# Five fewer matmuls on zeros at the head, and the small constants loaded behind the first piece of x

## The chip, the cores and the metric

The kernel runs on one core of a Trainium2 chip. Its time is the device time in microseconds (us) of one execution, and the median of several executions is compared. Five engines work side by side and meet only at semaphores: PE (TensorE, matrix products), DVE (VectorE), ACT (ScalarE), POOL (GpSimd) and SP (SyncE, which here only issues DMAs).

## What is computed

The input x is 1024 tokens of 512 float32 values. Two residual steps follow each other:

```python
x = x + attn(cond(x, itok_B_0_7, cond_W, cond_Wr, cond_A, cond_B), ...)
x = x + ffn(cond2(x, itok_B_0_23, cond2_W, cond2_b, lora_As, lora_Bs), ...)
```

`cond` is the stage that matters here. It computes the plain product `base = x @ W.T`, and beside it router logits `x @ Wr.T` with a bias for the language id of the batch, keeps the two largest of eight experts, and adds their rank-16 updates, weighted by a softmax, to `base`. `attn` is a polynomial approximation plus a gated feed-forward, `cond2` a product with an adapter chosen by id, and `ffn` a second gated feed-forward with low-rank parts. All of it is float32.

## The kernel before

The tokens are cut into two halves of 512 columns. x lies transposed in chunks of 128 channels, so the tile `X` has eight pieces, called here x00 to x03 for the first half and x10 to x13 for the second, each 128x512 float32 (256 KB). The weight of `cond` comes in four pieces of the same size, w0 to w3, one for each chunk of channels.

Every float32 operand is split into a high part, copied by ACT into a rounded format, and a low part, which DVE makes by subtracting the high part from the original. A product then takes three matmuls (low times high, high times low, high times high). ACT and DVE thus stand between every DMA and every matmul: a piece lands, ACT copies it, DVE subtracts, PE may use it. All copies carry line 541 and all subtractions line 911, since helpers record them.

The order at the head is written out by hand in the list `FIRST` (line 66): x00, w0, x01, x02, x03, w1, x10, x11, w2, x12, x13, w3. Three engines follow it in order. SP issues the loads in this order, from line 470 on. ACT makes the high parts in this order (line 567), with one addition: right behind the two copies of w0 it waits for `small_in`, the semaphore of the tile `sm`, and copies the router weight `WR` out of `sm` (lines 576 and 577). DVE makes the low parts in the same order, with `WR` in the same place (line 986). Only then do both go on to x01.

POOL issues three loads of small constants as the first things it does: `sm` (128 rows of 191 values, 95.5 KB; router weight, bias, identity matrix and more), `idb` (language ids, 4 KB) and `slot_i` (adapter ids). Its next instruction waits for `slots_ok` (line 500), which DVE makes out of `slot_i` at line 1006.

PE begins with `WARM` matmuls of 128x128 in bfloat16 on a tile of zeros (line 1502), which need only the memset of line 974. Their results are used by nobody. Then follow `base_0(0)` (12 matmuls on x00 and w0; the first three at lines 1510, 1512 and 1514), the logits of the first half (seven matmuls, lines 1455, 1458 and 1453, which need `WR` and x00 to x03), `base_0(1)` (12 matmuls on x01 and w1), the logits of the second half, and so on. The matmuls of `product` stand at lines 1435, 1436 and 1437. The core of PE's order at the head:

```python
base_0(0)
pe.wait_ge(wr_ready, 1)
for k in range(KC):
    pe.wait_ge(x_ready, x_count(0, k))
    logits(0, k)
base_0(1)
```

`base_0(1)` waits for `w_ready`, which DVE raises with the low part of w1.

Of the kernel before, what the change touches and what calls it, by code (L numbers as in the profile page):

```python
# [37 lines left out]
P_AP = P_GATE + 1  # L38
P_FFN = P_AP + 1 + ORDERS
RING = 4  # L40
WARM = 39


KS = 96
# [120 lines left out]
def build(nc, x, ids_b, slot_ids, small, pieces, parts, lora_a, lora_b, stk_up, out):  # L165
    with ExitStack() as ctx:
# [3 lines left out]
        def sem(name):  # L170
            return ctx.enter_context(nc.semaphore(name))
# [82 lines left out]
        x_in = [[sem(f"x_in{h}{c}") for c in range(KC)] for h in range(HALVES)]  # L254
# [82 lines left out]
        def raw_slot(p):  # L337
            k = (0, 1, 6, 7, 2, 3)[SLOT[p]]
            return raw[:, k, :]

        def raw_count(p):
            return 16 * SLOT[:p + 1].count(SLOT[p])

        def before_in_slot(p):

            return max([q for q in range(p) if SLOT[q] == SLOT[p]] or [P_TWO[LAST - 1]])
# [52 lines left out]
        def sum_region(q):  # L399
            a = SUM_AT[q % 2]  # L400
            return raw_flat[:, a:a + 1024]

        def merge_region(q):
            a = 3072 * (q % 2)
            return raw_flat[:, a:a + 1024]

        def merged_by_dma(q):

            return q - F2 - 1
# [58 lines left out]
        @block.sync  # L468
        def _(sp):
            for kind, h, c in FIRST:  # L470
                if kind == "x":
                    sp.dma_start(X[:, h, c, :], x[h, c]).then_inc(x_in[h][c], 16)
                else:
                    sp.dma_start(raw_slot(P_CW + c), pieces[P_CW + c]).then_inc(raw_in[SLOT[P_CW + c]], 16)
            for p in range(RING, PIECES):
                k, q = BLOCK_PIECES[p - P_FFN] if P_FFN <= p < P_S13 else (None, None)
                if k == 1:
                    if q > 1:
                        sp.wait_ge(w_ready, P_TWO[q - 2] + 1)
                    sp.dma_start(sum_region(q), parts[q][:, 0:1024]).then_inc(sum_in[q % 2], 16)  # L480
                sp.wait_ge(w_ready, before_in_slot(p) + 1)
                if k == 0:
                    a11 = slice(256 * (q % 2), 256 * (q % 2) + 256)
                    sp.dma_start(raw_slot(p)[:, a11], pieces[p][:, a11]).then_inc(raw_in[SLOT[p]], 16)
                else:
                    sp.dma_start(raw_slot(p), pieces[p]).then_inc(raw_in[SLOT[p]], 16)
            for n, (h, c, cols, _) in enumerate(OUTPUTS):

                sp.wait_ge(out_ready, n + 1)
                sp.dma_start(out[h, c, :, cols], X[:, h, c, cols]).then_inc(out_done, 16)  # L490
            sp.wait_ge(out_done, 16 * len(OUTPUTS))


        @block.gpsimd
        def _(pool):
            pool.dma_start(sm[:], small).then_inc(small_in, 16)
            pool.dma_start(idb[:], ids_b).then_inc(ids_in, 16)
            pool.dma_start(slot_i[:], slot_ids).then_inc(slots_in, 16)

            pool.wait_ge(slots_ok, 1)  # L500
            for b in range(BATCH):
                s = pool.value_load(slot_ok[0:1, b:b + 1], min_val=0, max_val=SLOTS - 1)
                pool.dma_start(ga_raw[:, b * KC * RANK:(b + 1) * KC * RANK], lora_a[s]).then_inc(lora_a_in, 16)
            pool.dma_start(su_raw[:], stk_up[0]).then_inc(su_in, 16)

            def sums_by_dma(q):

                k, n, at = q % 2, q // 2 + 1, SUM_AT[q % 2]
                pool.wait_ge(sum_in[k], 16 * n)
                pool.dma_start(raw_flat[:, at:at + 768], parts[q][:, 1024:1792], accum_op=ALU.add).then_inc(sum_two[k], 16)  # L510

            for q in range(F2):
                sums_by_dma(q)
            pool.wait_ge(g_ready, G_SPLIT[0, TAIL - 1, "T4"])
            for b in range(BATCH):
                s = pool.value_load(slot_ok[0:1, b:b + 1], min_val=0, max_val=SLOTS - 1)
                for row in (b % TILES * RANK, KB + b % TILES * RANK):
                    pool.dma_start(gb_raw[row:row + RANK, b // TILES, :], lora_b[s]).then_inc(lora_b_in, 16)
            def su_load(q):
                pool.wait_ge(su_ready, q)  # L520
                pool.dma_start(su_raw[:], stk_up[q]).then_inc(su_in, 16)

            def merge_by_dma(q):
                for p in (P_ONE[q], P_TWO[q]):
                    pool.wait_ge(raw_in[SLOT[p]], raw_count(p))
                pool.wait_ge(delta_out, merged_by_dma(q))
                pool.dma_start(merge_region(q), delta[:], accum_op=ALU.add).then_inc(merged_in, 16)

            for q in range(1, 3):
                su_load(q)  # L530
            for q in range(F2 + 2, END + 1):
                if q in (F2 + 5, F2 + 9, F2 + 11):
                    su_load({F2 + 5: 3, F2 + 9: 4, F2 + 11: 5}[q])
                merge_by_dma(q)
# [897 lines left out]
        def _(pe):  # L1432
# [67 lines left out]
            pe.wait_ge(warm_ready, 1)  # L1500
            for _ in range(WARM):
                pe.matmul(PB[LOGITS[1]][:, 0:P], warm[:], warm[:], start=True, stop=True)  # L1502
# [436 lines left out]
```

## Time and profile before

| | us |
|---|---|
| median of 3 runs (439.1 to 440.13) | 439.77 |
| the profiled execution | 439.4 |
| its span, first to last instruction | 437.7 |
| PE busy | 433.9 (99% of the span) |
| DVE, ACT, POOL busy | 347.3, 242.1, 40.6 |

The profile is of one execution. Its span and its time differ by 1.7 us, which lie outside of the instructions. A row of the timeline gives the start of a group, the time from its start to its end, the engine, the line, the operation with its output and input, and the count; where the engine sat idle before, the idle time and what ended it stand in brackets. SPq and POOLq are the instruction queues of these engines. The busy time of PE comes from modelled ends of pipelined matmuls, which overlap; short waits of PE are therefore read from the distance of two starts and not from the busy time. A DMA's time to landing runs from its issue to the last of its semaphore increments.

### The profile page before, as it was taken

To read this page: it belongs to the slowest core of one execution; us is meant where nothing else is said; L and a number is where in the kernel's file an instruction comes from. 1 tells how busy PE (TensorE), PEld (TensorE's weight loads), DVE (VectorE), ACT (ScalarE), POOL (GpSimd) and SP (SyncE) were. 2 spreads that over 40 slices of the span, in tenths; PEclk is the share of its full clock that TensorE was granted. 3 is DMA by queue.
4 is the path that set the end of the run, shared out by engine and by line. 5 is a ranking of instruction groups with operands and counts; after the bars stand their busy time and mean duration, and the time that the engine had idled before them with its cause. 6 is when DMAs were issued, how large, how long until landed. Compare 5 with 4: busy or idle time off the path is not lost.

```text
span 437.7 us, 5667 instructions
## 1 busy us (share of the span) xinstructions
PE 433.9 (99%) x1969; PEld 357.2 (82%) x1969; DVE 347.3 (79%) x524; ACT 242.1 (55%) x364; POOL 40.6 (9%) x64
## 2 busy tenths in 40 slices
PE   8999999999999999999999999999999999999997
PEld 7788888888888888888888888888888888888886
DVE  4756699676888867987799589799988799988663
ACT  6455443427566446664574658586754566755520
POOL 1003200000000001003400000010001010010000
PEclk9999999999999999999999999999999999999999
DMA  8505800044555655565551024054645444444004
GB/s 276 166 0 155 234 16 1 9 123 104 130 126 130 175 131 128 130 152 144 156 171 49 18 67 97 0 121 98 146 89 137 121 105 107 96 97 100 21 13 180
DMA packets 22171, 47.26 MB, mean 108 GB/s; under 512 B 2880, under 2 KB 4944, under 8 KB 22144
## 3 DMA queue, kind: packets, MB, share of 16 engines
q1 hardware_dynamic: 16992, 32.51, 24.0%
q0 software_dynamic: 5152, 14.39, 17.9%
q8 instruction: 16, 0.26, 0.3%
q14 instruction: 11, 0.09, 0.1%
HBM read 37.98 MB, written 2.10 MB: 92 GB/s over the span
## 4 chain that ended last, share of the span: by engine, by line
PE 99%; DVE 0%; issue 0%; DVEq 0%
PE PS L1589 21%; PE PS L1591 21%; PE PS L1590 21%; PE PS L1435 10%; PE PS L1437 10%; PE PS L1436 10%; PE PS L1705 1%; PE PS L1502 1%; PE PS L1713 0%; PE PS L1455 0%; PE PS L1749 0%; PE PS L1765 0%; PE PS L1766 0%; PE PS L1453 0%; PE PS L1747 0%; PE PS L1722 0%
## 5 line engine op out<-in xcount | busy, mean ns | idle before, releaser
L1589 PE MATMUL PS<-HT,WU 128*128 128x512 f32 x294 | 114.9, 391 | 0.0
L1590 PE MATMUL PS<-HT,WU 128*128 128x512 f32 x294 | 114.5, 390 | 0.0
L1591 PE MATMUL PS<-HT,WU 128*128 128x512 f32 x294 | 114.4, 389 | 0.0
L541 ACT ACTIVATE WU<-raw 128x256 fp32r<-128x256 f32 (+2 forms) x60 | 56.4, 939 | 29.6 <-PE PS L1591 17.0
L911 DVE TENSOR_TENSOR WU<-raw,WU 128x256 fp32r<-128x256 f32 (+2 forms) x61 | 65.0, 1065 | 4.8 <-ACT WU L541 4.7
L541 ACT ACTIVATE PS<-PS 128x512 f32<-128x512 f32 x58 | 33.9, 584 | 61.8 <-PE PS L1591 38.7
L1589 PEld LDWEIGHTS PS<-HT,WU 128*128 128x128 f32 x294 | 55.2, 188 | 12.3 <-DVE PS L1114 1.0
L541 ACT ACTIVATE G<-T 128x512 fp32r<-128x512 f32 (+3 forms) x62 | 49.5, 810 | 28.2 <-DVE T L1152 14.0
L1591 PEld LDWEIGHTS PS<-HT,WU 128*128 128x128 f32 x294 | 55.2, 188 | 11.7
L1590 PEld LDWEIGHTS PS<-HT,WU 128*128 128x128 f32 x294 | 55.2, 188 | 11.0
L911 DVE TENSOR_TENSOR G<-T,G 128x512 fp32r<-128x512 f32 (+3 forms) x59 | 53.2, 914 | 12.3 <-ACT G L541 11.6
L1589 PE MATMUL PS<-G,WU 128*128 128x512 f32 x112 | 43.6, 389 | 0.0
L1590 PE MATMUL PS<-G,WU 128*128 128x512 f32 x112 | 43.6, 389 | 0.0
L1591 PE MATMUL PS<-G,WU 128*128 128x512 f32 x112 | 43.6, 389 | 0.0
L1118 DVE TENSOR_TENSOR T<-PS,T 128x512 f32<-128x512 f32 x29 | 19.9, 687 | 15.2 <-PE PS L1591 15.2
L696 ACT ACTIVATE T<-PS 128x512 f32<-128x512 f32 x42 | 24.9, 592 | 12.4 <-PE PS L1591 12.4
L1114 DVE TENSOR_TENSOR PS<-PS,T 128x512 f32<-128x512 f32 x29 | 20.2, 695 | 9.4 <-ACT T L541 7.4
L1435 PE MATMUL PS<-G,WU 128*128 128x512 f32 x68 | 26.5, 390 | 0.0
L1437 PE MATMUL PS<-G,WU 128*128 128x512 f32 x68 | 26.5, 389 | 0.0
L1436 PE MATMUL PS<-G,WU 128*128 128x512 f32 x68 | 26.5, 389 | 0.0
L510 POOL DMA_DIRECT2D raw<-in_parts x14 | 12.1, 863 | 145.5 <-DMA raw<-in_parts 145.5
L1591 PEld LDWEIGHTS PS<-G,WU 128*128 128x128 f32 x112 | 21.0, 188 | 4.4
(169 smaller groups left out, 694.5 us busy)
## 6 DMA issues: line engine op xcount, KB each, us to landing
raw<-in_pieces SPq DMA_DIRECT2D x73, 256.0 KB, 3.0
raw<-in_parts SPq DMA_DIRECT2D x14, 512.0 KB, 3.7
raw<-delta POOLq DMA_DIRECT2D x13, 512.0 KB, 5.5
raw<-in_parts POOLq DMA_DIRECT2D x14, 384.0 KB, 5.0
X<-in_x SPq DMA_DIRECT2D x8, 256.0 KB, 5.6
raw<-in_pieces SPq DMA_DIRECT2D x14, 128.0 KB, 2.5
out_x<-X SPq DMA_DIRECT2D x7, 256.0 KB, 2.0
su_raw<-in_stk_up POOLq DMA_DIRECT2D x6, 192.0 KB, 5.8
```

Of the source, the lines that this page charges most:

```text
L510: pool.dma_start(raw_flat[:, at:at + 768], parts[q][:, 1024:1792], accum_op=ALU.add).then_inc(sum_two[k], 16)
L541: return nc.scalar.activation(o, i, ACT.Copy)
L696: nc.scalar.activation(T[:, h, :], bank, ACT.Silu).then_inc(silu[h], 1)
L911: return V.tensor_tensor(dst, full, f32(hi), ALU.subtract)
L1114: V.tensor_tensor(bank_b(q), bank_b(q), T[:, 4, :], ALU.add).then_inc(added_b, 1)
L1118: V.tensor_tensor(T[:, 5, :], bank_c(q), T[:, 4, :], ALU.add).then_inc(added_d, 1)
L1435: pe.matmul(o, w[:, 1, cols], xx[:, 0, :], start=start, stop=False)
L1436: pe.matmul(o, w[:, 0, cols], xx[:, 1, :], start=False, stop=False)
L1437: return pe.matmul(o, w[:, 0, cols], xx[:, 0, :], start=False, stop=stop)
L1589: pe.matmul(bank, w[:, 1, cols], hi, start=start and kc == 0, stop=False, skip_group_check=not start)
L1590: pe.matmul(bank, w[:, 0, cols], low, start=False, stop=False, skip_group_check=not start)
L1591: mm = pe.matmul(bank, w[:, 0, cols], hi, start=False, stop=kc == 1, skip_group_check=not start)
```

## The change

PE makes 34 matmuls on zeros instead of 39. POOL waits for the landing of x00 before it issues the three loads of small constants. Nothing else differs.

```diff
-WARM = 39
+WARM = 34
@@
         @block.gpsimd
         def _(pool):
+
+            pool.wait_ge(x_in[0][0], 16)
             pool.dma_start(sm[:], small).then_inc(small_in, 16)
             pool.dma_start(idb[:], ids_b).then_inc(ids_in, 16)
             pool.dma_start(slot_i[:], slot_ids).then_inc(slots_in, 16)
```

## Rows read from the trace of the kernel before

**Rows 1.** The page: the chain that ended last, its share by engine.
```profile
PE 99%; DVE 0%; issue 0%; DVEq 0%
```

**Rows 2.** The timeline of PE, the head up to the second product.
```profile
1.11 4.34 PE L1502 MATMUL PS<-warm 128*128 128x128 bf16 x39 [1.11 <-DVE warm L974]
5.21 0.77 PE L1510 MATMUL PS<-HT,G 128*128 128x512 f32 x1
5.79 0.46 PE L1512 MATMUL PS<-HT,G 128*128 128x512 f32 x1
6.08 0.39 PE L1514 MATMUL PS<-HT,G 128*128 128x512 f32 x1
...
6.31 0.40 PE L1435 MATMUL PS<-HT,G 128*128 128x512 f32 x1
```

**Rows 3.** The timeline of PE, the last logits and the first matmuls of `base_0(1)`.
```profile
8.39 0.40 PE L1455 MATMUL PS<-HT,WR 128*16 128x512 f32 x1
...
9.79 0.39 PE L1453 MATMUL PS<-HT,WR 128*8 128x512 f32 x1
...
10.02 0.40 PE L1455 MATMUL PS<-HT,WR 128*16 128x512 f32 x1
...
10.30 0.47 PE L1435 MATMUL PS<-HT,G 128*128 128x512 f32 x1
```

**Rows 4.** The timeline of ACT, its copies at the head.
```profile
3.48 0.63 ACT L541 ACTIVATE HT<-X 128x512 fp32r<-128x512 f32 x1 [1.12 <-DMA X<-in_x]
4.25 0.31 ACT L541 ACTIVATE G<-raw 128x128 fp32r<-128x128 f32 x1
...
6.09 0.23 ACT L541 ACTIVATE WR<-sm 128x32 fp32r<-128x32 f32 x1 [1.11 <-DMA sm<-in_small]
6.86 1.88 ACT L541 ACTIVATE HT<-X 128x512 fp32r<-128x512 f32 x3 [0.54 <-DMA X<-in_x]
8.79 0.63 ACT L541 ACTIVATE G<-raw 128x512 fp32r<-128x512 f32 x1
```

**Rows 5.** The timeline of DVE, its subtractions at the head and the ids.
```profile
4.75 0.82 DVE L911 TENSOR_TENSOR G<-raw,G 128x128 fp32r<-128x128 f32 x2
6.35 0.19 DVE L911 TENSOR_TENSOR WR<-sm,WR 128x32 fp32r<-128x32 f32 x1 [0.79 <-ACT WR L541]
7.53 1.95 DVE L911 TENSOR_TENSOR HT<-X,HT 128x512 fp32r<-128x512 f32 x3 [0.98 <-ACT HT L541]
9.46 0.69 DVE L911 TENSOR_TENSOR G<-raw,G 128x512 fp32r<-128x512 f32 x1
12.15 1.38 DVE L911 TENSOR_TENSOR G<-X,G 128x512 fp32r<-128x512 f32 x2
14.12 0.17 DVE L989 CAST idf<-idb 128x8 f32<-128x8 int32 x1
33.76 0.15 DVE L1003 CAST slot_f<-slot_i 1x8 f32<-1x8 int32 x1
```

**Rows 6.** The timeline of POOL at the head, and its time to landing for `sm`.
```profile
1.42 0.70 POOL L496 DMA_DIRECT2D sm<-in_small  x1 [0.86 <-POOLq L1929]
2.12 0.58 POOL L497 DMA_DIRECT2D idb<-in_ids_b  x1
2.67 0.55 POOL L498 DMA_DIRECT2D slot_i<-in_slot_ids  x1
...
DMA to landing us min/median/max: 4.6/4.6/4.6
```

**Rows 7.** Issue to landing of later POOL loads: `in_lora_b`, `in_lora_a`, `in_stk_up` (32, 32, 192 KB).
```profile
DMA to landing us min/median/max: 1.9/2.6/4.5
...
DMA to landing us min/median/max: 2.2/2.9/5.9
...
DMA to landing us min/median/max: 2.6/5.8/6.6
```

**Rows 8.** Busy time by stretch; the last three columns are granted clock, DMA share, GB/s.
```profile
3.00:3.50 0.50, 0.50 (x8) 0.50 (x6) 0.00 (x0) 0.02 (x1) 0.22 (x1) 1.00 1.06 401
3.75:4.75 1.00, 1.00 (x12) 1.00 (x11) 0.61 (x2) 0.85 (x3) 0.00 (x0) 1.00 0.76 185
8.00:12.00 4.00, 4.00 (x19) 2.28 (x18) 4.00 (x7) 3.77 (x7) 0.00 (x0) 1.00 1.05 402
```

## The prediction

> **What bounds the kernel now.** I read the chain that ended last first. It is PE for 99% of the span [rows 1], so a microsecond in which PE has no work is a microsecond of the result, and one saved at the head stays saved only if PE's next operand is there as early. The edits touch the first ten microseconds alone, so I read those in the timeline, engine by engine.
>
> PE starts on zeros at 1.11 and its 39 matmuls end at 5.45; the first real one starts at 5.21, as the weights are loaded ahead, and the next at 5.79, 6.08 and 6.31 [rows 2]. (5.45 - 1.11 - 0.31 for the last one alone) over 38 distances is 0.106 us for 128 columns, which is the 1.2 GHz level. The starts of the 512-column matmuls are 0.57, 0.29 and 0.23 apart: 0.23 is the 2.4 GHz level, so the clock rises at about 5.9, within the second real matmul. (The column of the granted clock reads 1.00 for the head too [rows 8]; the distances contradict it there, and I go by them.) Then 0.23 apart all along, until the last logits matmul at 10.02. The next would start at 10.25, but starts at 10.30 [rows 3], because the low part of w1 is done only at 9.46 + 0.69 = 10.15 [rows 5]. So at this place PE and the split of w1 arrive together: whichever becomes later sets the start of `base_0(1)`. After it there is room: the low part of x13 ends at 13.53 [rows 5], while its logits matmuls follow the 12 of `base_0(1)` and five others, at 10.30 + 17 x 0.23 = 14.2.
>
> What makes w1 late? ACT copies it at 8.79 right behind x01, x02 and x03 (from 6.86), and before them it stood idle twice: 1.11 us for `sm`, until 6.09, and 0.54 us for x01 [rows 4]. The DMAs ran at 401 GB/s until POOL's loads came in and at 185 GB/s from 3.75 to 4.75, and at 402 again from 8 to 12 [rows 8]. This is what the second edit aims at.
>
> **Five matmuls fewer.** 5 x 0.106 = 0.53 us. The first real matmul would start at 5.21 - 0.53 = 4.68. Its inputs are there: the copy of w0's first part ends at 4.25 + 0.31 = 4.56 [rows 4]. But it now runs at the lower level: 128 columns take 0.106, so 512 take 0.43. Starts: 4.68, 4.68 + 0.57 = 5.25, 5.68; if the clock rises at 5.9 as before, the third is half done by then and the fourth starts at about 6.01 instead of 6.31. It needs the second part of w0, done at 4.75 + 0.82 = 5.57 [rows 5]. So 0.30 of the 0.53 us remain, PE is through with the logits at 9.95 instead of 10.25, and waits there for w1. Alone this edit is worth 0.00 to 0.05 us, since w1 at 10.15 covers it. The bounds of its worth with w1 out of the way are 0.30 and, had the clock risen before 4.7, 0.53.
>
> **The loads of the constants.** What moves is all three issues on POOL, 0.70, 0.58 and 0.55 us [rows 6]. x00 is there at 3.48, when ACT starts on it [rows 4]; with some 0.05 for the wait the issue of `sm` starts at 3.53 instead of 1.42, 2.1 later. `idb` and `slot_i` move as much. With the 4.6 us to landing of `sm`, `idb` landed at 6.7 and will at 8.8, and is wanted at 14.12; `slot_i` will at 9.4 and is wanted at 33.76 [rows 5, 6]; POOL itself has nothing else to do before `slots_ok`. What hides these two is the splitting of x and w on DVE, and they would cost only if they were some 5 us later than that. `sm` is not hidden: ACT stands at it in order, and x01, x02, x03 and w1 are queued behind it on ACT, then on DVE, and PE waits for these.
>
> The one unknown is `sm`'s time from issue to landing in its new place. It was 4.6 [rows 6]. POOL's later loads span 1.9 to 6.6 [rows 7]: 1.9 to 3 when little else moves, up to 5.9 for 32 KB when SP's loads run beside them. At 3.5 to 8 us SP's queue is as full as it was at 1.4 to 6, so I take 4.6, the nearest row by place, size and neighbours, and keep 2.6 to 5.9 for the range.
>
> Then `sm` lands at 3.53 + 4.6 = 8.15, and x01 to w1 have landed by then or soon after, as SP's queue ran free meanwhile. ACT copies `WR` from 8.18 and is at x01 at 8.18 + 0.26 = 8.44 (was 6.86). Three copies at the pace of (1.88 - 0.63) / 2 = 0.62 bring w1's copy to 10.30 and its end to 10.93, DVE's part ends 0.73 later, at 11.66 (the same 0.73 as from 9.42 to 10.15), and `base_0(1)` starts 0.15 later, at 11.8 instead of 10.30. That is +1.5 us. PE meanwhile ends `base_0(0)` at about 8.1 and then has only seven matmuls to do until 11.8, some 2 us idle in pieces. The part of DVE that follows keeps pace: five more subtractions at 0.69 [rows 5] bring x13 to 15.1, and it is wanted at 11.8 + 17 x 0.23 = 15.7. From there on PE is bound by itself as before, so the shift goes through to the end.
>
> In general the shift at `base_0(1)` is (time to landing - 4.6) + 1.5, and never below 9.95 - 10.30 = -0.35, where PE itself is the limit. The second edit swallows all that the first gives unless the landing takes under 3.1 us.
>
> **A rule weighed.** `sm` took 4.6 us for 95.5 KB [rows 6]. The Trainium skill, page "DMA: Bandwidth & Descriptors", section "Anatomy of one DMA", fits a load issued from GpSimd as 2.0 us plus its bytes over 436 GB/s; by it this one takes 2.2, an estimate, and lands at 5.8. This trace does not agree for a load with neighbours, and does for the fastest of the small ones (1.9 to 2.6). The case is the rival "quick landing" below, which is worked out from rows.
>
> **The rivals.**
> Quick landing (the other side: no loss or a gain). If POOL's load meets less traffic in its new place, it may land like the fastest later ones, 2.6 to 3 us [rows 7], at 6.1 to 6.5. ACT is at x01 by 6.4 to 6.8, w1's copy ends at 8.9 to 9.3 and `base_0(1)` can start at 9.8 to 10.2; PE arrives at 9.95. Shift -0.35 to -0.1, time 439.05 to 439.3. It needs w1 to have landed by 8.3, which it would at the 401 GB/s of [rows 8]. For it: the medians of the two sets of 32 KB loads are under 3 us [rows 7]. Against it: they are a third of `sm`'s size and were spread over calmer stretches, while at the head the DMA share is 0.76 to 1.06 [rows 8]. It decides below 3.1 us of landing.
> Middle: landing in 3.0 to 4.3 us. Shift -0.1 to +1.2, time 439.3 to 440.6. The same mechanism with milder crowding.
> Crowded: SP has issued more by 5.6 than by 3.5, so the load may take 5.2 to 6.6 like the slowest in [rows 7]; shift +2.1 to +3.5, time 441.5 to 442.9.
> Clock: with some 2 us of idle time in pieces between 8.1 and 11.8 PE might be given the lower level again. Before, it worked at that level from 1.11 to 5.9, 4.8 us; the same again would cost half of it, 2.4 us, 443.3 in all. No stretch of before shows such a fall, and the idle pieces are shorter than 1.2 us each, so it is unlikely.
>
> **How the numbers follow.** Against the profiled execution: 439.4 + 1.5 = 440.9. That execution lies 0.37 below the median of 439.77. Part of such a difference between runs can be the moment of the clock's rise, which moves PE but not ACT's chain, and a PE that waits at `base_0(1)` swallows it; if all of it is of another kind, the median is 441.3. I take 440.9. Chances: forecast (landing 4.3 to 5.2, 440.6 to 441.5) 0.42; crowded 0.15; clock 0.05; middle 0.26; quick 0.12. The range leaves out the clock and the ends of crowded and of quick: 439.1 to 442.3. A measurement of this kernel can tell some 0.2%, 0.9 us, from no change. Slower by more than that is above 440.65: most of the forecast (0.35 of its 0.42, as the head's own scatter blurs its edge), crowded and clock, 0.55. Faster by more is below 438.9, which even the quick landing reaches only if the clock rises early: 0.05. The same: 0.40.
>
> **What would show it.** Right: POOL issues `sm` at about 3.5; ACT's idle time before `WR` grows from 1.1 to 3.2 and the idle time before x01 vanishes; x01 to x03 land earlier than before; PE starts its first real matmul at 4.7 and `base_0(1)` at 11.8 with gaps among the logits; from there every start is 1.5 later. Wrong: if `sm` lands within 3.1 us, `base_0(1)` starts at or before 10.3; if w1 itself lands later than 10, DMAs and not ACT's order set the start; if 512-column matmuls behind 8 us are 0.43 apart, it is the clock.

## The result and the profile after

| | us |
|---|---|
| before, median of 6 executions (438.91 to 440.13) | 439.37 |
| changed, median of 6 executions (441.52 to 443.08) | 441.91 |
| ratio, 95% interval | 1.0064, 1.0052 to 1.0077 |
| changed, the profiled execution and its span | 441.52, 439.8 |

The change makes the kernel 0.64% slower, 2.5 us between the medians and 2.1 us between the two profiled executions. The forecast was 440.9, which is 1.5 us above this median of before and 1.0 us below the measured one. Lines behind the second edit are numbered two higher than before.

POOL in the timeline of the changed kernel, and issue to landing of `sm`; it answers [rows 6]:

```profile
3.80 0.70 POOL L498 DMA_DIRECT2D sm<-in_small  x1 [3.23 <-DMA X<-in_x]
4.49 0.57 POOL L499 DMA_DIRECT2D idb<-in_ids_b  x1
5.05 0.54 POOL L500 DMA_DIRECT2D slot_i<-in_slot_ids  x1
...
DMA to landing us min/median/max: 5.1/5.1/5.1
```

ACT at the head of the changed kernel, which answers [rows 4]:

```profile
3.51 0.63 ACT L543 ACTIVATE HT<-X 128x512 fp32r<-128x512 f32 x1 [1.15 <-DMA X<-in_x]
...
8.95 0.23 ACT L543 ACTIVATE WR<-sm 128x32 fp32r<-128x32 f32 x1 [3.94 <-DMA sm<-in_small]
9.08 1.66 ACT L543 ACTIVATE HT<-X 128x512 fp32r<-128x512 f32 x3
10.64 0.62 ACT L543 ACTIVATE G<-raw 128x512 fp32r<-128x512 f32 x1
```

ACT now idles 3.94 us for `sm`, against 1.11, and the 0.54 us that it waited for x01 are gone: x01 landed while ACT stood at `sm`. PE in the changed kernel, which answers [rows 2, 3]:

```profile
1.11 3.81 PE L1504 MATMUL PS<-warm 128*128 128x128 bf16 x34 [1.11 <-DVE warm L976]
4.74 0.76 PE L1512 MATMUL PS<-HT,G 128*128 128x512 f32 x1
...
7.87 0.40 PE L1439 MATMUL PS<-HT,G 128*128 128x512 f32 x1
...
9.46 0.41 PE L1457 MATMUL PS<-HT,WR 128*16 128x512 f32 x1 [1.19 <-DVE WR L913]
...
10.47 0.40 PE L1455 MATMUL PS<-HT,WR 128*8 128x512 f32 x1 [0.38 <-DVE HT L913]
...
12.37 0.47 PE L1437 MATMUL PS<-HT,G 128*128 128x512 f32 x1
```

The first real matmul starts 0.47 us earlier (4.74 against 5.21), `base_0(0)` ends 0.3 us earlier, then PE idles for `WR` and among the logits, and `base_0(1)` starts at 12.37 instead of 10.30. This shift of 2.07 us is all but the whole 2.1 us between the profiled executions. The chain that ended last, in order of time, says it in five lines (start, length, what; "issue" is time without a releaser in the profile):

```profile
0.87 2.62 DMA X<-in_x
3.49 0.31 issue
3.80 5.12 DMA sm<-in_small
...
9.18 0.53 ACT HT L543
...
9.73 0.70 DVE HT L913
```

Before, this chain was PE from 1.11 on; now a DMA of 95.5 KB is on it for 5.12 us.

### The profile page after: what moved, and what is told of

Its sections match the earlier page's. It is cut to its first block, busy times and chain, and to the rows that moved or that the text cites. A ratio compares the mean times of both kernels' runs of the same rounds, so it can differ in the third digit from the quotient of the medians.

```text
span 439.8 us, 5657 instructions
## 1 busy us (share of the span) xinstructions
PE 434.4 (99%) x1964; PEld 356.5 (81%) x1964; DVE 346.8 (79%) x524; ACT 241.2 (55%) x364; POOL 40.7 (9%) x64
## 4 chain that ended last, share of the span: by engine, by line
PE 97%; DMA 2%; DVE 0%; ACT 0%; issue 0%; DVEq 0%
PE PS L1591 21%; PE PS L1592 21%; PE PS L1593 21%; PE PS L1437 10%; PE PS L1438 10%; PE PS L1439 9%; PE PS L1707 1%; DMA sm<-in_small 1%; DMA X<-in_x 1%; PE PS L1715 0%; PE PS L1455 0%; PE PS L1751 0%; PE PS L1768 0%; PE PS L1767 0%; PE PS L1457 0%; PE PS L1749 0%
## 5 line engine op out<-in xcount | busy, mean ns | idle before, releaser
L1120 DVE TENSOR_TENSOR T<-PS,T 128x512 f32<-128x512 f32 x29 | 19.9, 687 | 15.2 <-PE PS L1593 15.2
```

Source lines behind the costliest of these rows:

```text
L1120: V.tensor_tensor(T[:, 5, :], bank_c(q), T[:, 4, :], ALU.add).then_inc(added_d, 1)
```

## The experiments

Each is compared with executions of the kernel before on the same chip; their median was 439.33 to 439.45.

**One edit at a time.** `WARM = 34` alone:

```diff
-WARM = 39
+WARM = 34
```

> The first edit alone: 34 matmuls on zeros, the loads of the constants at once as before. Theory (ACT's place of the constants sets the start of base_0(1), w1 is split no earlier): PE is at the end of the logits 0.3 us earlier and waits there for w1, base_0(1) starts within 0.1 us of 10.3, time within 0.3 us of before. Rival (fewer zeros cost by themselves, as the clock rises later or falls back): base_0(1) at 10.8 or later, time 0.5 us or more above before.

Measured: median 439.24 (438.91 to 439.6) against 439.45, ratio 0.9997 (0.9989 to 1.0006). No measurable effect. In its profiled execution `base_0(1)` started at 9.76, outside of the expected 0.1 us around 10.3. There `sm` landed after 3.9 us, 0.7 less than in the profile of before, and the clock also rose earlier (the second real matmul starts 0.31 us behind the first, not 0.58). Whether the edit has a part in either is not shown; the median does not move. The rival is out. The wait alone:

```diff
+            pool.wait_ge(x_in[0][0], 16)
             pool.dma_start(sm[:], small).then_inc(small_in, 16)
```

> The second edit alone: 39 matmuls on zeros, POOL waits for x00. Theory: the constants land at about 8.9, base_0(1) starts at about 12.4, time as with both edits, 2.1 us above before in most executions. Rival (the two edits cost together, the early first product makes the gap longer and it is the gap that costs): under 1.5 us above before.

Measured: median 441.87 (441.52 to 444.09), ratio 1.0063 (1.0045 to 1.0082), the loss of both edits together. In its profile `sm` took longer than expected, 6.3 us, and `base_0(1)` moved with it, to 13.62 where about 12.4 was expected. ACT, PE and issue to landing of `sm` with the wait alone:

```profile
10.19 0.23 ACT L543 ACTIVATE WR<-sm 128x32 fp32r<-128x32 f32 x1 [5.22 <-DMA sm<-in_small]
...
13.62 0.47 PE L1437 MATMUL PS<-HT,G 128*128 128x512 f32 x1
...
DMA to landing us min/median/max: 6.3/6.3/6.3
```

From `WR`'s copy to `base_0(1)` it is 3.43 us here and 3.42 in the changed kernel: a fixed chain behind a landing that varies.

**Which load it is.** `sm` at once as before, and only the lists of ids wait for x00:

```diff
             pool.dma_start(sm[:], small).then_inc(small_in, 16)
+            pool.wait_ge(x_in[0][0], 16)
             pool.dma_start(idb[:], ids_b).then_inc(ids_in, 16)
```

> 34 matmuls on zeros; POOL issues sm at once as before, and only the two lists of ids wait for x00. Theory: sm lands at 5.4 to 6.1 as before, time within 0.3 us of before, and the whole loss of the change belongs to sm. Rival (the small loads of ids disturb SP's loads, in their old place and in the new one): x01 lands by 5.6, time 0.4 us or more below before.

Measured: median 439.23 (438.83 to 439.73), ratio 0.9998 (0.9989 to 1.0007). `sm` landed after 4.2 us, ACT idled 0.71 us for it. The whole loss is `sm`'s.

**A later wait.** POOL waits for w0:

```diff
-            pool.wait_ge(x_in[0][0], 16)
+            pool.wait_ge(raw_in[0], 16)
```

> Both edits, but POOL waits for w0, which lands 0.77 us behind x00. Theory (every 1 us of delay of the constants' issue is 1 us at base_0(1)): issue at about 4.6, time to landing 5.1 again, base_0(1) at 13.1, fastest execution 0.8 us above that of both edits, 442.3; the longer idle time of PE lets the clock fall more often. Rival (the time to landing shrinks when the queue of SP has moved on): less than 0.4 us above both edits.

Measured: median 443.76 (443.4 to 445.38), ratio 1.0109 (1.0092 to 1.0126). The fastest execution lies 1.9 us above the fastest with both edits, where 0.8 was expected. `sm` was issued at 4.60, 0.80 later, and took 5.7 us, 0.6 longer. The rest is in these lines. PE with the wait for w0, and then busy time by stretch (the third number from the right is the granted clock):

```profile
10.81 0.41 PE L1457 MATMUL PS<-HT,WR 128*16 128x512 f32 x1 [2.68 <-DVE WR L913]
...
13.50 0.63 PE L1455 MATMUL PS<-HT,WR 128*8 128x512 f32 x1
13.93 0.63 PE L1457 MATMUL PS<-HT,WR 128*16 128x512 f32 x1
14.36 0.63 PE L1437 MATMUL PS<-HT,G 128*128 128x512 f32 x1
```

```profile
8.00:11.80 3.80, 0.77 (x3) 0.10 (x2) 0.91 (x3) 1.50 (x4) 0.00 (x0) 1.00 1.05 385
11.80:15.20 3.40, 3.37 (x8) 1.61 (x9) 3.40 (x6) 3.40 (x8) 0.00 (x0) 0.50 0.31 86
15.20:18.00 2.80, 2.80 (x14) 2.01 (x13) 2.73 (x7) 2.23 (x6) 0.00 (x0) 0.99 0.40 147
```

The granted clock fell to 0.50, the 1.2 GHz level, from 11.8 to 15.2, after a stretch of 3.80 us in which PE was busy for 0.77, and the matmuls start 0.43 apart in it. All five executions have a granted clock of 0.992 to 0.996 in the mean over the span.

**PE's idle time filled with zeros.** `zeros(n)` makes n more matmuls of 128 columns on the tile of zeros. First in the changed kernel:

```diff
             base_0(0)
+            zeros(20)
             pe.wait_ge(wr_ready, 1)
             for k in range(KC):
+                if k:
+                    zeros(4)
                 pe.wait_ge(x_ready, x_count(0, k))
                 logits(0, k)
+            zeros(4)
```

> Both edits, and matmuls on zeros put into PE's idle time: 20 behind base_0(0), 4 before each further logits step, 4 behind the last; nothing but the zeros is added to what is computed. Theory (the two executions at 443.0 with a mean clock of 0.996 come from the clock falling in PE's idle time): no execution has a clock under 0.998 and none is 1 us or more above its fastest; the fastest stays at 441.5 to 441.8, as the constants land no earlier. Rival (the slow ones come from a later landing): executions at 443 are still there.

Measured: 441.30, 442.03, 442.36, 442.37 and 442.47, all five with a mean clock of 1.000. So the half of the expectation on the clock held. The half on the spread failed: three of the five are 1.06 to 1.17 us above the fastest, at full clock, and the median of 442.36 is no lower than without the zeros; the fastest, 441.30, is just under the expected 441.5 to 441.8. Without them, two of six executions of the changed kernel have a mean clock of 0.996 and took 443.03 and 443.08, and one of six with the wait alone has it too and took 444.09, the slowest of each set. Three of twelve against none of five does not settle it, so the filling was repeated where the fall had been seen, in the kernel that waits for w0 (the same edit with `zeros(40)` behind `base_0(0)`):

> POOL waits for w0 as in the run with that wait alone (443.76, where the clock fell in PE's idle time), and PE's idle time is filled with matmuls on zeros: 40 behind base_0(0), 4 before each further logits step and 4 behind the last; only zeros are added to what is computed. Theory (the fall of the clock costs up to 1 us on top of the late constants): no 512-column matmul of the head behind 8 us is 0.43 apart, the median falls by 0.7 to 1.2 us to 442.6 to 443.1, and none is above 443.6. Rival (the late landing is all of it): the median stays within 0.4 us of 443.76.

Measured: median 443.05 (442.56 to 443.59) against 443.76 (443.4 to 445.38) without the zeros, and mean clocks of 0.999 to 1.000 against 0.992 to 0.996. The same stretches with the zeros:

```profile
8.00:11.80 3.80, 3.50 (x46) 2.68 (x44) 0.35 (x2) 0.94 (x3) 0.00 (x0) 1.00 1.02 377
11.80:15.20 3.40, 3.26 (x26) 1.85 (x26) 3.40 (x6) 3.40 (x8) 0.00 (x0) 1.00 0.07 25
```

The clock stays at 1.00, although `sm` landed even later than without the zeros (ACT began `WR` at 10.86 against 10.30). So the fall is real and costs 0.7 us of the median there (0.6 if each is taken from the executions of before on its own chip); and the late table is the larger part.

**Why the load takes 5 us.** Both edits, and SP holds x03 and all behind it until `sm` has landed (`n` counts the entries of `FIRST`):

```diff
+                if n == 4:
+                    sp.wait_ge(small_in, 16)
                 if kind == "x":
                     sp.dma_start(X[:, h, c, :], x[h, c]).then_inc(x_in[h][c], 16)
```

> Both edits, and SP waits for sm's landing before it issues x03 and all that follow it. Theory (sm waits behind SP's queued loads): with only x01 and x02 queued, its time to landing falls from 5.1 to 3.0 to 3.6. Rival (5 us is this load's own time in any company once POOL waited): 4.6 to 5.3 again. The time is no test, as x03 and w1 land late: about 442.

Issue to landing of `sm`, and ACT, with SP held back:

```profile
DMA to landing us min/median/max: 3.1/3.1/3.1
...
6.96 0.23 ACT L545 ACTIVATE WR<-sm 128x32 fp32r<-128x32 f32 x1 [1.87 <-DMA sm<-in_small]
7.09 1.14 ACT L545 ACTIVATE HT<-X 128x512 fp32r<-128x512 f32 x2
9.67 0.63 ACT L545 ACTIVATE HT<-X 128x512 fp32r<-128x512 f32 x1 [1.44 <-DMA X<-in_x]
```

With nothing queued by SP behind x02 the same load takes 3.1 us instead of 5.1. The two executions took 441.97 and 441.47, as now x03 and w1 are late.

This run alone does not tell whether `sm` shares the DMA engines with what SP issues or stands behind it. The packets do. Here are the packets, MB and share of SP's queue from the start of the span up to the last 0.2 us step before the first packet of POOL's queue: before (to 3.4), changed (to 7.2), POOL waiting for w0 (to 8.6), SP held back (to 5.2):

```profile
q1 hardware_dynamic: 236, 0.45, 44.3%
...
q1 hardware_dynamic: 939, 1.73, 73.7%
...
q1 hardware_dynamic: 1145, 2.10, 74.9%
...
q1 hardware_dynamic: 544, 1.01, 63.7%
```

When `sm` was issued, SP had issued x00 and was issuing w0 (before, at 1.42); it had issued six pieces and was at the seventh (changed, at 3.80), had issued eight (wait for w0, at 4.60), or stood still behind four (held back, at 3.86). A piece is 0.26 MB, so that makes up to 0.52, 1.57 to 1.84, 2.10 and 1.05 MB. In all four `sm`'s first packet moved only when about as much as SP had issued ahead of it had moved. From there to the landing it was 1.7 us in the last three and 2.6 before. The load stood behind the pieces in front of it; from issue to first packet it was 3.4 us in the changed kernel, 2.0 before and 1.3 with SP held back.

**Whose place costs: the table's or the pieces'.** Both edits, with `WR` behind w1 on ACT and DVE, and `base_0(1)` ahead of the logits on PE (the copy and subtraction of `WR` stand under `if (kind, c) == ("w", 1)` in both loops):

```diff
             base_0(0)
+            base_0(1)
             pe.wait_ge(wr_ready, 1)
             for k in range(KC):
                 pe.wait_ge(x_ready, x_count(0, k))
                 logits(0, k)
-            base_0(1)
```

> Both edits, with WR's copy and subtraction put behind those of w1 on ACT and DVE, and the logits of the first half behind base_0(1) on PE; the computation is the same. Theory (the loss is ACT's order: x01 to w1 have landed and stand behind the wait for sm): x01 is copied at about 5.6, w1 at about 7.8, base_0(1) starts at 9.3 instead of 12.4, logits follow at 12.1, and the pair ends at 13.7 instead of 15.2: fastest executions 440.0 to 440.3, 1.3 to 1.5 us under both edits. Rival (the crowded DMAs hold x01 to w1 back as well): 441 or more.

Measured: median 440.57 (440.27 to 440.94), ratio 1.0027 (1.0017 to 1.0038). ACT and PE with the router last:

```profile
5.93 1.26 ACT L543 ACTIVATE HT<-X 128x512 fp32r<-128x512 f32 x2 [0.88 <-DMA X<-in_x]
7.53 0.63 ACT L543 ACTIVATE HT<-X 128x512 fp32r<-128x512 f32 x1 [0.33 <-DMA X<-in_x]
8.14 0.63 ACT L543 ACTIVATE G<-raw 128x512 fp32r<-128x512 f32 x1
9.70 0.23 ACT L543 ACTIVATE WR<-sm 128x32 fp32r<-128x32 f32 x1 [0.93 <-DMA sm<-in_small]
...
9.64 0.47 PE L1439 MATMUL PS<-HT,G 128*128 128x512 f32 x1 [1.48 <-DVE G L914]
```

w1's copy starts at 8.14 instead of 10.64 although `sm` lands later still (9.70), and the median falls by 1.34 us. The pieces had been there; they stood behind the table. What is left of the loss, 1.2 us, is PE's idle time of 1.48 us for w1, which has no logits to cover it any more, less the 0.3 by which `base_0(0)` ends earlier.

**Is there something to gain at the head?** `sm` loaded by SP behind w0, POOL's two lists when `sm` is there:

```diff
                     sp.dma_start(raw_slot(P_CW + c), pieces[P_CW + c]).then_inc(raw_in[SLOT[P_CW + c]], 16)
+                    if c == 0:
+                        sp.dma_start(sm[:], small).then_inc(small_in, 16)
```

> 34 matmuls on zeros; the table sm is loaded by SP right behind w0, and POOL waits for it before it loads the two lists of ids. Theory (ACT's wait for sm, and the 5 us that a POOL load takes beside SP's loads, are what costs): sm lands below 5.2, ACT idles for it under 0.3 us, x01 lands at about 5.5 and w1 at 7.3 to 7.8, base_0(1) starts where PE arrives, 9.9 to 10.0 if the clock rises at 5.9; time 0.2 to 0.6 us below before. Rival (the head of before is already at its limit, whoever loads sm): within 0.1 us of before.

Measured: median 439.17 (438.89 to 440.36), ratio 0.9997 (0.9988 to 1.0006). The table was there in time (2.9 us to landing, ACT did not wait), but ACT stood idle for x01 until 5.99, for x02 until 7.33 and for x03 until 8.37, came to w1 at 9.02, later than expected, and `base_0(1)` started at 10.53. The theory's gain did not come. Two more runs ask whether POOL's lists are to blame: the same with the lists behind x10, and `sm` by POOL as before with the lists behind x10 (`pool.wait_ge(x_in[1][0], 16)` ahead of them in both).

> 34 matmuls on zeros, sm loaded by SP behind w0, and POOL waits for x10 before it loads the two lists of ids, so that none of POOL's loads moves beside x00 to w1. Theory (POOL's loads slow SP's down): w1 lands by 7.8 instead of 9.0, base_0(1) starts where PE arrives, at most 10.0, time 0.2 to 0.6 us below before. Rival (SP's loads are no faster without POOL's): w1 lands at 8.5 or later, time within 0.15 us of before.

> 34 matmuls on zeros, sm at once by POOL as before, and the two lists of ids wait for x10. Theory (the lists disturb SP's loads): w1 lands by 8.2 and base_0(1) starts at 10.0 or before, time 0.1 to 0.4 us below before. Rival: as before, within 0.1 us.

Measured: 439.32 (438.88 to 439.64), ratio 0.9998 (0.9989 to 1.0007), and 439.35 (438.9 to 439.87), ratio 1.0001 (0.9992 to 1.001). In time the rivals hold in both. With SP's table and no load of POOL's before 9.8, w1's copy started at 8.45, 0.34 earlier than in [rows 4]; that lies between the 7.8 of the theory and the 8.5 of the rival, and ACT was busy with x03 until then, so w1's own landing is not told by it. With only the lists moved it started at 8.79, as before. In the first of the two PE did not wait for w1 at all; its rows:

```profile
9.12 0.69 DVE L913 TENSOR_TENSOR G<-raw,G 128x512 fp32r<-128x512 f32 x1
...
10.07 0.40 PE L1457 MATMUL PS<-HT,WR 128*16 128x512 f32 x1
10.30 0.39 PE L1437 MATMUL PS<-HT,G 128*128 128x512 f32 x1
```

The low part of w1 is there at 9.81, and PE starts `base_0(1)` at 10.30 because it comes no earlier: in this execution the matmuls of the first product start 0.43 apart, the lower clock level, from 5.31 to 6.59, and in before only until 5.9. The earliest `base_0(1)` in any profile is 9.76, 0.54 ahead of before, and none of these versions is measurably better than before.

## Why the prediction was right, and where its sum was off

**The bound and the meeting point** were read rightly: PE and w1 meet at `base_0(1)`, and the shift there (2.07 us) is the shift of the end (2.1 us).

**The five zeros** were put at 0.00 to 0.05 us alone. The run with them alone shows no measurable difference. Within the changed kernel the three first starts came at 4.74, 5.30 and 5.73 against the forecast 4.68, 5.25 and 5.68.

**The moved loads.** The lists cost nothing, as forecast; the run with only them moved shows it. For `sm` the mechanism was right and three sizes were off:

| term | forecast | measured |
|---|---|---|
| x00 landed to issue of `sm` | 0.05 | 0.31 (3.49 to 3.80) |
| issue to landing | 4.6 | 5.12 |
| landing to `base_0(1)` | 3.65 | 3.45 |
| start of `base_0(1)` | 11.8 | 12.37 |

Together +0.57 us. The copies followed each other at (1.66 - 0.63) / 2 = 0.52 us and not at 0.62, so ACT ran ahead; then DVE, whose subtractions started 0.60 apart (9.73 to 11.54 for three), set the start. The step that was furthest off is "SP's queue is as full as it was": SP had issued up to two pieces in front of the load at 1.42 and six to seven at 3.80, and the load's first packet moved after 0.45 MB of SP's in the one case and 1.73 in the other. With the queue held back the load takes 3.1. For the profiled execution `sm`'s own 4.6 was still nearer than the 5.9 of a small load beside SP's stream [rows 7]; over the four profiles in which `sm` waits for x00 and SP is not held, it is the other way round (mean 5.5). The rule of the Trainium skill, page "DMA: Bandwidth & Descriptors", section "Anatomy of one DMA", by which 2.2 us is the estimate, is not met by any of POOL's loads of `sm` here, and the run nearest to it is the one with the queue held back, at 3.1. A slip without effect: the logits of a half are eight matmuls in the trace, not seven, and six of them, not five, precede those that need x13.

The landing also varies from one execution to the next: with the wait for x00 it was 5.1, 6.3, 4.8 and 5.7 in four profiles (both edits, the wait alone, filled with zeros, router last). Where it is late, the end goes with it. Span minus start of `WR`'s copy:

| | span | `WR` at | difference |
|---|---|---|---|
| before | 437.7 | 6.09 | 431.6 |
| both edits | 439.8 | 8.95 | 430.9 |
| the wait alone | 441.0 | 10.19 | 430.8 |
| both edits, filled | 439.6 | 8.51 | 431.1 |
| wait for w0, filled | 441.9 | 10.86 | 431.0 |
| wait for w0 | 442.1 | 10.30 | 431.8 |

Four kernels with a late table lie within 0.3 us of 431, over 2.4 us of landings. Before lies some 0.7 higher, as there `sm` is not what sets the end: the end was bound by PE from 1.11 on. The wait for w0 lies 0.8 above its filled twin: the fallen clock.

**The clock** was given a chance of 0.05, on the ground that the idle pieces were short, and this was too little. Two of six executions of the changed kernel have a mean clock of 0.996, the value of the run in whose trace the fall is seen, and they are the two slowest. No trace of these two is there to show the fall; that filling keeps the clock up was shown for the wait for w0, and of ten filled executions none is below 0.999. The price was too high: 2.4 us forecast, 0.6 to 0.8 measured. Half of the 3.4 us at the lower level would be 1.7; a likely reason for the difference, not tested, is that some of the slowed matmuls would have waited for DVE anyway.

The median of 441.91 is thus the forecast plus 0.6 us of mis-sized terms, and some 0.4 us that the median lies above the profiled execution, for which later landings and the fallen clock are the likely cause. It lies outside of the forecast's own 440.6 to 441.5 and in the stretch of the rival "crowded" (441.5 to 442.9, chance 0.15), whose mechanism, more issued by SP, is what the packets show; it was inside the range, but the forecast as a number was low. The landing of 5.1 us in the profiled execution still belongs to the forecast's own 4.3 to 5.2; the landings of 6.3 and 5.7 in the other profiles belong to the rival's. The rival of a quick landing was wrong: no load of `sm` behind x00 came under 4.8 us while SP's queue ran, and even those issued at 1.42 took 3.9 to 4.8.

## What to carry to other kernels

A small load that an in-order engine meets early belongs ahead of the large ones, however little bandwidth is won by moving it: what counts is not what its bytes cost the others but who is queued behind its landing. Before such a move, count the bytes that the other queue has issued ahead of the load in its new place, as they move first, and follow the waiting engine's list to the first operand that the bound engine lacks. Here five of 39 filler matmuls ahead of the first operand could be cut for nothing, and nothing was gained by it, as another operand set the next start.

## What the runs showed of the hardware that was not expected

A load issued by POOL stood behind what SP had issued before it, although the two have queues of their own: the first packet of `sm` moved when SP's queue had moved 0.45, 1.01, 1.73 and 2.10 MB, with up to two, four, six to seven and eight pieces of 0.26 MB issued ahead of it. The 95.5 KB took 4.8 to 6.3 us when issued behind x00 or w0, 3.9 to 4.8 when issued at 1.42, and 3.1 with SP held back.

In the run that waits for w0, TensorE's granted clock fell to 0.50 from 11.8 to 15.2 although PE had never been idle for more than 2.7 us at a stretch and was busy again before the fall; 128x512 matmuls then started 0.43 us apart instead of 0.23.

Moving all of POOL's loads out of the way let ACT start on w1 only 0.3 us earlier (8.45 against 8.79).
